# Fewer, larger transfers for the attention stacks, and a new order of the late ones in the SP queue

## The chip, the cores and the metric

One core of a Trainium2 chip runs the whole program. The metric is the device time of one execution in microseconds (us); lower is better.

## The reference

The input x is 2 x 1024 x 256 in f32. xn is its layer norm. The result is x + s * g, where s is attention and g a gated mixture of experts, both fed with xn:

```python
proj = xn @ in_proj.T + in_proj_bias            # q, k, v: 16 heads of 16
scores = einsum('bhqd,bhkd->bhqk', q, k) * SCALE + rel * alibi_slopes   # causal
attn = maximum(softmax(scores), 1e-10)
s = einsum('bhqk,bhkd->bhqd', attn, v) ... @ out_w.T + out_b
# _ffn: rms norm, router over 32 experts, top 4, capacity 128,
#       silu(gate) * up, down, plus a shared expert of 704 columns
g = silu(xn + experts + shared)
x = x + s * g
```

## The kernel before

The work after a prologue is a pipeline over 32 units. Unit k is one attention head (16 heads of batch 0, then 16 of batch 1) and also one expert. Four slots (`SLOTS`) hold the operands of four units. `phases` runs a `phase` function on each engine for k from -2 to 32; on SP the first and the last ones are written out and 24 of them are six turns of a loop over four.

In phase k, in eight steps s, TensorE (PE) does pass 1 of head k + 2 (scores in rows of queries, L765; VectorE takes the row maximum L1342, ScalarE the exponential and its sum L1062), pass 2 of head k (scores again, transposed, with the row's shift as three extra rows of the operand; mask L787, product L791, exponential L1071, clamp L1348) and the values of head k - 1 (L810, L813). Between them lie the expert's steps: transpose of the gathered rows `XE` (L838), gate and up (L850), down (L868), the shared expert (L889, L897).

The precision of f32 is kept with bf16 parts. The operand of a head (`QS`, `KS`, 111 rows of 1024 bf16 in the tile STACKS) is six blocks of 16 rows, taken from the three parts of q or k in DRAM in a fixed order (q: 0, 1, 2, 0, 1, 0; k: 0, 0, 0, 1, 1, 2), and 15 rows for position. The first three of these 15 on the q side are overwritten with the head's shift rows: GpSimd (POOL) works them out, PE flips them (L832), VectorE copies them to CT as 24 rows of 128 (L1361), and SP sends CT to rows 96 to 98 of the stack (`store_shift`, L569). Pass 2 of head k waits for that at its first step (`c_rows_ready`, L775).

All plain loads and stores are issued by SP, one after the other, in the order that is written. In phase k SP issues, each with its wait ahead of it:

1. the stack of head k + 3 (`load_stack`, L497 and L498), after pass 2 of head k - 1;
2. the weights of expert k + 5 (`load_expert`, L514 to L518), after the down product of expert k + 1;
3. in phase 31, the eight loads of the experts' sum (`load_experts_sum`, L610);
4. the attended rows of head k - 1 (`store_heads`, L586), after their copy to OEV (L1407); for the last eight heads they go straight into the tile ATTS (named XN in the profile), for the others to `att_rows` in DRAM;
5. the shift rows of head k + 1 (`store_shift`), after the copy to CT;
6. in phase 25 `load_again(0)`: 1 MB of attended rows of batch 0 into ATTS (L596) and the copy of x of batch 0 to the output, 1 MB from DRAM to DRAM (L597); in phase 26 `load_again(1)`: the attended rows of batch 1 so far (L599) and x of batch 1 (L601).

POOL gathers the rows of expert k + 3 in phase k with an indirect DMA (L1624). In the last phases PE projects the attended rows (L907), the experts' sum is gated on ScalarE and VectorE (`tanh_sum`, `gate`, `last_sum`, L1423), POOL adds the first half to the output and SP stores the second.

In the prologue the bf16 parts of q and k are made in 16 tasks on a ring of four buffers (`RING`) and stored by SP (`store_parts`, L481). A task waits until its buffer's store has landed (L1027). The stores 8 to 11 stand in SP's queue with the stack loads of heads 0 and 1 between them; then come stores 12 to 15, the stacks of heads 2 and 3, and the first four experts.

Of the kernel before, what the change touches and what calls it, by code (L numbers as in the profile page):

```python
# [25 lines left out]
P = 128  # L26
# [5 lines left out]
H = 16  # L32
# [59 lines left out]
DIRECT = UNITS - NQ  # L92

# [14 lines left out]
def build(nc, x, in_proj, in_b, out_w, out_b, slopes, w_norm, w_router, w_gate, w_up, w_down,  # L108
          sw_gate, sw_up, sw_down, w_sg, out):
    ctx = ExitStack()  # L110
    with ctx:
# [316 lines left out]
        def _(sp):  # L428
# [65 lines left out]
            def load_operand(t, rows, plan, alibi, u_head, u, semaphore):  # L494
                one = rows[:, bass.ds(u_head, DH), :]
                for r, part in enumerate(plan):
                    sp.dma_start(t[r * DH:(r + 1) * DH, :], one[part]).then_inc(semaphore, 16)  # L497
                sp.dma_start(t[SHIFT:ROWS, :], alibi[bass.ds(u, 1)].rearrange("a r s -> (a r) s"))\  # L498
                    .then_inc(semaphore, 16)

            def load_queries(u_head, u, slot):
                load_operand(QS[slot], q_parts, (0, 1, 2, 0, 1, 0), q_alibi, u_head, u, stack_loaded[slot])

            def load_keys(u_head, u, slot):
                load_operand(KS[slot], k_parts, (0, 0, 0, 1, 1, 2), k_alibi, u_head, u, stack_loaded[slot])
# [37 lines left out]
            def phase(it, k):  # L543
# [45 lines left out]
            def load_again(b):  # L589

                heads = H if b == 0 else DIRECT
                for r in range(SLOTS):
                    sp.wait_ge(o_stored[r], 64 * (heads // SLOTS + 1))
                if b == 0:
                    sp.wait_ge(moe_started, 32)
                    sp.dma_start(ATTS[:, :, 0, :], att_rows[0:D].rearrange("(a p) t -> p a t", p=P)).then_inc(att_loaded[0], 16)  # L596
                    sp.dma_start(out[0], x[0]).then_inc(x_again[0], 16)  # L597
                else:
                    sp.dma_start(ATTS[:, 0, 1, :], att_rows[D:D + P]).then_inc(att_loaded[1], 16)  # L599
# [1125 lines left out]
```

## Time and profile before

| | us |
|---|---|
| median of 3 runs (lowest, highest) | 638.89 (635.98, 642.01) |
| the profiled execution, own time | 641.21 |
| its span from first to last instruction | 639.6 |
| PE busy | 564.7 (88%) |
| VectorE busy | 489.6 (77%) |
| ScalarE busy | 445.3 (70%) |
| GpSimd busy | 263.8 (41%) |
| granted TensorE clock, mean | 0.961 |

Engines in the rows: PE matmuls, PEld weight loads (they run beside PE), DVE VectorE, ACT ScalarE, POOL GpSimd, SPq the queue of SP, which only issues transfers. What an engine idled for stands in square brackets behind a row, with what ended it.

### The profile page before, as it was taken

The page shows a single profiled execution, that of the slowest core. Times are in us where ns is not written, and L with a number is a line of the kernel's source. Part 1 is how long each engine was busy: PE and PEld are TensorE (multiplying, and loading weights), DVE is VectorE, ACT ScalarE, POOL GpSimd, SP SyncE. Part 2 cuts the span into 40 slices and gives each one's busy share as a digit, 9 for nine tenths or more (in the row PEclk, how much of TensorE's full clock was granted, in tenths as well). Part 3 has the DMA queues.
Part 4 walks back from the last instruction along what each step waited for, and adds up shares of the span by engine and source line. Part 5 has one row for each costly group of instructions (what it writes and reads, how often), then busy time and mean ns, then how long its engine had stood idle before and what let it go on. Part 6 is the DMA issues. An engine that isn't in the chain of part 4 may idle for free.

```text
span 639.6 us, 17284 instructions
## 1 busy us (share of the span) xinstructions
PE 564.7 (88%) x4583; PEld 386.8 (60%) x4584; DVE 489.6 (77%) x1098; ACT 445.3 (70%) x1021; POOL 263.8 (41%) x632
## 2 busy tenths in 40 slices
PE   1699559778998999999999999999999998999994
PEld 1594227545665666666666666666666665666663
DVE  5988963668778778886887788778878885788556
ACT  1412574268877778887888788888878886788670
POOL 7630000215445355445544564455355445344403
PEclk9959869799999999999999999999999999999998
DMA  8992255553335333533543344335334346731157
GB/s 243 179 241 76 97 156 167 136 161 60 91 84 111 86 92 87 107 89 90 102 104 98 87 102 90 87 84 116 90 89 102 92 103 200 167 80 24 16 146 136
DMA packets 79538, 71.47 MB, mean 112 GB/s; under 512 B 18115, under 2 KB 70021, under 8 KB 79493
## 3 DMA queue, kind: packets, MB, share of 16 engines
q1 hardware_dynamic: 70292, 59.30, 34.1%
q0 software_dynamic: 9136, 11.80, 12.3%
q8 instruction: 12, 0.20, 0.1%
q14 instruction: 18, 0.14, 0.1%
q10 hardware_dynamic: 80, 0.03, 0.0%
HBM read 47.82 MB, written 23.59 MB: 112 GB/s over the span
## 4 chain that ended last, share of the span: by engine, by line
PE 50%; ACT 14%; issue 11%; DVE 10%; DMA 7%; SPq 6%; ACTq 1%; POOL 1%; POOLq 0%; DVEq 0%
ACT PSB L1062 7%; PE PSB L897 6%; PE PSB L765 6%; PE PSB L791 6%; ACT PB L1071 5%; PE PSB L889 5%; PE PSB L813 5%; PE PSB L810 4%; PE PSB L868 4%; PE PSB L787 3%; SPq L497 2%; PE PSB L666 2%; PE PSB L761 2%; PE PSB L850 2%; DVE WDS L1277 2%
## 5 line engine op out<-in xcount | busy, mean ns | idle before, releaser
L1342 DVE TENSOR_REDUCE NEGM<-PSB 128x1 f32<-128x1024 f32 (+7 forms) x256 | 192.3, 752 | 64.4 <-PE PSB L765 62.5
L1062 ACT ACTIVATE PSB<-PSB,NEGM 128x1024 f32<-128x1024 f32 (+7 forms) x256 | 182.5, 713 | 33.3 <-DVE NEGM L1342 33.0
L1071 ACT ACTIVATE PB<-PSB 128x128 f32<-128x128 f32 (+7 forms) x256 | 166.3, 651 | 43.7 <-PE PSB L791 41.6
L1348 DVE TENSOR_SCALAR PB<-PB 128x128 f32<-128x128 f32 (+7 forms) x256 | 116.9, 466 | 26.5 <-ACT PB L1071 24.1
L765 PE MATMUL PSB<-STACKS 111*128 111x512 bf16 (+3 forms) x384 | 106.6, 332 | 0.0
L791 PE MATMUL PSB<-STACKS 111*128 111x512 bf16 (+3 forms) x384 | 104.3, 326 | 0.0
L787 PE MATMUL PSB<-MK,IDB 128*128 128x128 bf16 x256 | 57.5, 225 | 21.2 <-ACT PSB L1062 13.7
L1660 POOL DMA_INDIRECT moe_rows<-YE,IDX x32 | 57.3, 1792 | 29.2 <-issue 29.2
L810 PE MATMUL PSB<-PB,VH 128*32 128x256 f32 x640 | 68.3, 387 | 0.0
L787 PEld LDWEIGHTS PSB<-MK,IDB 128*128 128x128 bf16 x256 | 24.5, 96 | 58.4 <-ACT PB L1071 31.5
L761 PE MATMUL PSB<-MQ,IDB 128*128 128x128 bf16 x256 | 58.3, 228 | 1.1 <-ACT UL L1049 0.5
L813 PE MATMUL PSB<-PB,VH 128*32 128x128 f32 x1024 | 55.6, 275 | 0.8 <-DVE PB L1348 0.7
L1620 POOL COPY IDX<-TABS 128x2 int32 (+1 forms) x32 | 20.3, 634 | 79.9 <-DVE VS L1333 79.9
L1624 POOL DMA_INDIRECT XES<-xf_rows,IDX x32 | 38.2, 1193 | 32.5 <-POOL IDX L1620 29.7
L1062 ACT ACTIVATION_READ_ACCUMULATOR PSB<-PSB,NEGM 128x1 f32 x256 | 51.5, 201 | 0.0
L897 PE MATMUL PSB<-SWD,HS 128*128 128x256 f32 x192 | 50.6, 391 | 0.0
L850 PE MATMUL PSB<-WGU,XES 128*128 128x352 f32 x128 | 48.9, 462 | 1.8 <-issue 1.8
L813 PEld LDWEIGHTS PSB<-PB,VH 128*32 128x32 f32 x1024 | 47.1, 109 | 4.6 <-issue 1.4
L1566 POOL TENSOR_TENSOR CR<-LSUM,LEX 128x8 f32<-128x8 f32 x32 | 6.5, 202 | 98.9 <-ACT LEX L1077 98.9
L897 PEld LDWEIGHTS PSB<-SWD,HS 128*128 128x128 f32 x192 | 33.7, 188 | 12.1 <-issue 8.6
L791 PEld LDWEIGHTS PSB<-STACKS 111*128 111x128 bf16 x384 | 32.6, 99 | 12.9 <-issue 0.3
L761 PEld LDWEIGHTS PSB<-MQ,IDB 128*128 128x128 bf16 x256 | 24.7, 97 | 24.5 <-issue 8.9
(199 smaller groups left out, 1169.4 us busy)
## 6 DMA issues: line engine op xcount, KB each, us to landing
STACKS<-q_parts SPq DMA_DIRECT2D x192, 32.0 KB, 1.8
STACKS<-k_parts SPq DMA_DIRECT2D x192, 32.0 KB, 1.8
WGU<-in_L_ffn_w_gate_dram SPq DMA_DIRECT2D x32, 176.0 KB
WGU<-in_L_ffn_w_up_dram SPq DMA_DIRECT2D x32, 176.0 KB
WDS<-in_L_ffn_w_down_dram SPq DMA_DIRECT2D x32, 176.0 KB
q_parts<-PB SPq DMA_DIRECT2D x8, 384.0 KB, 2.6
XN<-in_L_attn_qkv_dram SPq DMA_DIRECT2D x4, 512.0 KB, 6.0
moe_rows<-XN SPq DMA_DIRECT2D x1, 2048.0 KB, 8.7
```

Of the source, the lines that this page charges most:

```text
L761: pe.matmul(psf[:, base + i * P:base + w], IDB[:, :], MQ[:, :], start=True, stop=False, skip_group_check=True)
L765: ins = pe.matmul(psf[:, base + c0:base + c1], q, KS[slot][0:ROWS, c0:c1], start=(c1 < w), stop=True, skip_group_check=True)
L787: pe.matmul(psf[:, base:base + P], IDB[:, :], MK[:, :], start=True, stop=False, skip_group_check=True)
L791: ins = pe.matmul(psf[:, base + c0:base + c1], key, QS[slot][0:ROWS, j * P + c0:j * P + c1], start=(c0 > 0), stop=True, skip_group_check=True)
L810: ins = pe.matmul(o, v, probs[:, c - j:far - j + 1:far - c, :], start=False, stop=(j == 0), skip_group_check=True)
L813: ins = pe.matmul(o[:, 1, :], v, probs[:, far - j, :], start=(far == j), stop=False, skip_group_check=True)
L850: ins = pe.matmul(o[:, 0:2 * F], XET[:, part, :], WGU[slot][:, part, :], start=(part == 0), stop=(part == KC - 1))
L897: ins = pe.matmul(o[:, 0:D], HS[0:m, ch, which * P:(which + 1) * P], SWD[0:m, ch, :], start=(ch == 0), stop=(ch == NF - 1))
L1062: act.activation(sc, sc, ACT.Exp, bias=NEGM[:, par, i:i + 1], accum_out=LSUM[:, par, i:i + 1]).then_inc(exp1_done, 1)
L1071: act.activation(PB[:, k % 2, prob_offset(s):prob_offset(s) + (s + 1) * P], psf[:, base:base + (s + 1) * P], ACT.Exp).then_inc(exp2_done, 1)
L1342: dve.tensor_reduce(NEGM[:, par, i:i + 1], psf[:, base:base + (i + 1) * P], AX_X, ALU.max, negate=True).then_inc(max_ready, 1)
L1348: dve.tensor_scalar(p, p, FLOOR, 0.0, ALU.subtract, ALU.max).then_inc(clamp_done, 1)
```

## The change

Three edits, all in what SP issues:

- A stack operand is loaded in four transfers in place of seven: runs of parts that stand side by side (q: 0-1-2, 0-1, 0) or are repeated (k: 0 three times, 1 twice, 2) become one transfer each, the repeated ones with a source that is broadcast. A whole stack takes 8 in place of 14. The bytes are the same.
- In a phase, `store_shift` stands ahead of `store_heads`, and is one transfer of CT to the three rows in place of three.
- `load_again` becomes five pieces in phases 25 to 29: ATTS of batch 0 in two halves (25, 26), ATTS of batch 1 (27), x of batch 1 in two halves (28, 29). The copy of x of batch 0 becomes eight transfers of 128 rows, one in each phase 2, 6, ..., 30 (`copy_x`), behind the attended rows.

```diff
+AGAIN = range(DIRECT + 1, DIRECT + 6)
-            def load_operand(t, rows, plan, alibi, u_head, u, semaphore):
+            def load_operand(t, rows, runs, alibi, u_head, u, semaphore):
                 one = rows[:, bass.ds(u_head, DH), :]
-                for r, part in enumerate(plan):
-                    sp.dma_start(t[r * DH:(r + 1) * DH, :], one[part]).then_inc(semaphore, 16)
+                r = 0
+                for first, parts, times in runs:
+                    n = parts * times
+                    src = one[first:first + parts]
+                    if times > 1:
+                        src = src.broadcast_to([n, DH, S])
+                    sp.dma_start(t[r * DH:(r + n) * DH, :], src).then_inc(semaphore, 16)
+                    r += n
-                load_operand(QS[slot], q_parts, (0, 1, 2, 0, 1, 0), ...)
+                load_operand(QS[slot], q_parts, ((0, 3, 1), (0, 2, 1), (0, 1, 1)), ...)
-                load_operand(KS[slot], k_parts, (0, 0, 0, 1, 1, 2), ...)
+                load_operand(KS[slot], k_parts, ((0, 1, 3), (1, 1, 2), (2, 1, 1)), ...)
...
+                if exists(it, k + 1):
+                    store_shift(it, k + 1)
                 if exists(it, k - 1):
                     store_heads(it, k - 1)
-                if exists(it, k + 1):
-                    store_shift(it, k + 1)
-                if isinstance(it, int) and k == DIRECT + 1:
-                    load_again(0)
-                if isinstance(it, int) and k == DIRECT + 2:
-                    load_again(1)
+                if k >= 2 and k % SLOTS == 2:
+                    copy_x(it, k)
+                if isinstance(it, int) and k in AGAIN:
+                    load_again(k)
...
-                for a in range(3):
-                    sp.dma_start(rows[SHIFT + a:SHIFT + a + 1, :].rearrange("o (t q) -> o t q", q=P),
-                                 CT[NQ * a:NQ * a + NQ, :]).then_inc(c_rows_ready, 16)
+                sp.dma_start(rows[SHIFT:SHIFT + 3, :], CT[:, :]).then_inc(c_rows_ready, 16)
...
+            def copy_x(it, k):
+                rows = bass.ds(turn(it, k, SLOTS, P), P)
+                sp.dma_start(out[0][rows, :], x[0][rows, :]).then_inc(x_again[0], 16)
+
+            def load_again(k):
+                n = k - AGAIN[0]
+                if n < 3:
+                    heads = D // DH if n < 2 else DIRECT
+                    for r in range(SLOTS):
+                        sp.wait_ge(o_stored[r], 64 * (heads // SLOTS + 1))
+                    sp.wait_ge(moe_started, 32)
+                    sp.dma_start(ATTS[:, n % 2, n // 2, :], att_rows[n * P:(n + 1) * P]).then_inc(att_loaded[n // 2], 16)
+                else:
+                    t = NQ // 2 * (n - 3)
+                    sp.wait_ge(shared_added, 16 * (UNITS // SLOTS // 2))
+                    sp.dma_start(XAGAIN...[:, t:t + NQ // 2, :], x_t[:, NQ + t:NQ + t + NQ // 2, :]).then_inc(x_again[1], 16)
```

The counts that others wait for follow: a stack 8 transfers, shift rows 1, `att_loaded[0]` 2, `x_again[0]` 8, `x_again[1]` 2.

## Rows read from the trace of the kernel before

**Rows 1.** The page's chain that ended last, shares of the span by engine.
```profile
PE 50%; ACT 14%; issue 11%; DVE 10%; DMA 7%; SPq 6%; ACTq 1%; POOL 1%; POOLq 0%; DVEq 0%
```

**Rows 2.** Timeline of DVE, the copy to CT: start us, duration, once a unit.
```profile
202.49 0.21 DVE L1361 COPY CT<-PSB 24x128 bf16<-24x128 bf16 x1 [0.49 <-PE PSB L832]
218.93 0.21 DVE L1361 COPY CT<-PSB 24x128 bf16<-24x128 bf16 x1 [0.49 <-PE PSB L832]
...
309.36 0.21 DVE L1361 COPY CT<-PSB 24x128 bf16<-24x128 bf16 x1 [0.50 <-PE PSB L832]
323.89 0.21 DVE L1361 COPY CT<-PSB 24x128 bf16<-24x128 bf16 x1 [0.49 <-PE PSB L832]
338.25 0.21 DVE L1361 COPY CT<-PSB 24x128 bf16<-24x128 bf16 x1 [0.49 <-PE PSB L832]
353.27 0.21 DVE L1361 COPY CT<-PSB 24x128 bf16<-24x128 bf16 x1 [0.33 <-PE PSB L832]
368.77 0.21 DVE L1361 COPY CT<-PSB 24x128 bf16<-24x128 bf16 x1 [0.50 <-PE PSB L832]
...
531.50 0.21 DVE L1361 COPY CT<-PSB 24x128 bf16<-24x128 bf16 x1 [0.33 <-PE PSB L832]
550.85 0.21 DVE L1361 COPY CT<-PSB 24x128 bf16<-24x128 bf16 x1 [0.49 <-PE PSB L832]
566.17 0.21 DVE L1361 COPY CT<-PSB 24x128 bf16<-24x128 bf16 x1 [0.49 <-issue]
```

**Rows 3.** The chain in order of time at 533 us: start, duration.
```profile
533.20 8.62 DMA XES<-xf_rows,IDX
```

**Rows 4.** Timeline of SP's queue at 534 us.
```profile
534.50 0.62 SPq L597 DMA_DIRECT2D out_dram<-in_L_attn_qkv_dram  x1
```

**Rows 5.** Timeline of SP's queue at 201 us.
```profile
200.96 3.42 SPq L586 DMA_DIRECT2D att_rows<-OEV  x4
```

**Rows 6.** Who waited for the shift rows (L569) in all.
```profile
  PEld PSB L787: 8.8, 16
  PE PSB L787: 3.6, 4
```

**Rows 7.** Timeline of SP's queue in the prologue.
```profile
91.83 2.93 SPq L497 DMA_DIRECT2D STACKS<-q_parts  x6
```

**Rows 8.** The chain in order of time, store 11 of the parts.
```profile
103.55 4.27 DMA k_parts<-XES
```

**Rows 9.** Waits of PE over the whole span: total, times, longest.
```profile
PE PSB L733 <- DVE TS L1326: 2.0, 1, 2.0
```

**Rows 10.** Timeline of PEld, the first expert's gate and up.
```profile
130.66 0.30 PEld L850 LDWEIGHTS PSB<-WGU,XES 128*128 128x128 f32 x2 [2.31 <-issue]
```

**Rows 11.** Windows: PE, PEld, DVE, ACT, POOL busy, clock, DMA share of 16 engines, GB/s.
```profile
111.00:113.00 2.00, 2.00 (x11) 1.67 (x10) 2.00 (x2) 1.59 (x4) 0.00 (x0) 1.00 1.01 342
344.00:348.00 4.00, 4.00 (x29) 2.78 (x28) 3.64 (x8) 3.26 (x9) 0.88 (x5) 1.00 0.28 67
```

**Rows 12.** The tile XES, 320 to 335 us: one gather, its use, its landing.
```profile
L838 PEld LDWEIGHTS PSB<-IDF,XES x2: 141/142/143, 330.7 to 330.9; 128*128 128x128 f32 x2
L1624 POOL DMA_INDIRECT XES<-xf_rows,IDX x1: 1090/1090/1090, 326.2 to 326.2; - x1
DMA to landing us min/median/max: 3.1/3.1/3.1
```

**Rows 13.** Timeline of SP's queue at the end.
```profile
604.64 3.11 SPq L586 DMA_DIRECT2D XN<-OEV  x4
607.86 2.08 SPq L569 DMA_DIRECT2D STACKS<-CT  x3
610.07 3.98 SPq L610 DMA_DIRECT2D XFT<-moe_rows  x8
```

**Rows 14.** Timeline of DVE at the end.
```profile
606.93 0.21 DVE L1361 COPY CT<-PSB 24x128 bf16<-24x128 bf16 x1 [1.12 <-PE PSB L832]
619.23 0.69 DVE L1423 TENSOR_TENSOR XFT<-XFT,XNT 128x512 f32<-128x512 f32 x1 [0.79 <-DMA XFT<-moe_rows]
```

More of the change, by code:

```diff
@@ L501, in load_queries @@
             def load_queries(u_head, u, slot):
-                load_operand(QS[slot], q_parts, (0, 1, 2, 0, 1, 0), q_alibi, u_head, u, stack_loaded[slot])
+                load_operand(QS[slot], q_parts, ((0, 3, 1), (0, 2, 1), (0, 1, 1)), q_alibi, u_head, u, stack_loaded[slot])
             def load_keys(u_head, u, slot):
-                load_operand(KS[slot], k_parts, (0, 0, 0, 1, 1, 2), k_alibi, u_head, u, stack_loaded[slot])
+                load_operand(KS[slot], k_parts, ((0, 1, 3), (1, 1, 2), (2, 1, 1)), k_alibi, u_head, u, stack_loaded[slot])
             def load_stack(u_head, u, slot):
@@ L587, in store_heads @@
                         .then_inc(o_stored[k % SLOTS], 16)
[L589 to L594, printed above, removed]
+            def copy_x(it, k):
[7 more added lines that the diff above has]
+                        sp.wait_ge(o_stored[r], 64 * (heads // SLOTS + 1))
                     sp.wait_ge(moe_started, 32)
-                    sp.dma_start(ATTS[:, :, 0, :], att_rows[0:D].rearrange("(a p) t -> p a t", p=P)).then_inc(att_loaded[0], 16)
-                    sp.dma_start(out[0], x[0]).then_inc(x_again[0], 16)
+                    sp.dma_start(ATTS[:, n % 2, n // 2, :], att_rows[n * P:(n + 1) * P]).then_inc(att_loaded[n // 2], 16)
                 else:
-                    sp.dma_start(ATTS[:, 0, 1, :], att_rows[D:D + P]).then_inc(att_loaded[1], 16)
+                    t = NQ // 2 * (n - 3)
                     sp.wait_ge(shared_added, 16 * (UNITS // SLOTS // 2))
-                    sp.dma_start(XAGAIN.rearrange("p (t d) -> p t d", d=D), x_t[:, NQ:2 * NQ, :]).then_inc(x_again[1], 16)
+                    sp.dma_start(XAGAIN.rearrange("p (t d) -> p t d", d=D)[:, t:t + NQ // 2, :],
+                                 x_t[:, NQ + t:NQ + t + NQ // 2, :]).then_inc(x_again[1], 16)
             def load_experts_sum():
@@ L623, in _ @@
             sp.wait_ge(added_out, 16 * (NT // 4))
-            sp.wait_ge(x_again[0], 16)
+            sp.wait_ge(x_again[0], 16 * (UNITS // SLOTS))
         @block.tensor
@@ L750, in pass1 @@
                 if s == 0:
-                    pe.wait_ge(stack_loaded[slot], turn(it, k, SLOTS, 14 * 16, 14 * 16))
+                    pe.wait_ge(stack_loaded[slot], turn(it, k, SLOTS, 8 * 16, 8 * 16))
                 used = {0: -1, 1: 0, 2: 1, 3: 2, 4: 3, 5: 3, 6: 5, 7: 4}[s]
@@ L774, in pass2 @@
                 if s == 0:
-                    pe.wait_ge(c_rows_ready, unit(it, k, 48, 48))
+                    pe.wait_ge(c_rows_ready, unit(it, k, 16, 16))
                 if s == 4 and ahead:
@@ L914, in project @@
                     pe.wait_ge(exp1_done, UNITS * NQ)
-                    pe.wait_ge(att_loaded[0], 16)
+                    pe.wait_ge(att_loaded[0], 32)
                 if g == 1:
@@ L1359, in turn_shift @@
                 if k >= 1:
-                    dve.wait_ge(c_rows_ready, unit(it, k, 48))
+                    dve.wait_ge(c_rows_ready, unit(it, k, 16))
                 dve.tensor_copy(CT[:, :], PSB[0:3 * NQ, O_BANK, C_COL:C_COL + P // 2].bitcast(BF16))\
@@ L1442, in add_input @@
                 x_late = XAGAIN[:, 512 * n:512 * (n + 1)]
-                dve.wait_ge(x_again[1], 16)
+                dve.wait_ge(x_again[1], 32)
                 dve.wait_ge(fin_product, n + 1)
@@ L1693, in _ @@
             phases(pool, phase, 1)
-            pool.wait_ge(x_again[0], 16)
+            pool.wait_ge(x_again[0], 16 * (UNITS // SLOTS))
             out_t = out.rearrange("b (t p) d -> p (b t) d", p=P)
```

## The prediction

> **What bounds the kernel now.** I read the chain of waits first: half of it is PE's own work, ScalarE and VectorE carry 24%, and DMA with SP's queue 13% [rows 1]. So transfers are no bound of the whole, but there are places where they are. To find them I took one instruction that runs once a unit, the copy to CT, and read the distances [rows 2]. In the steady part four distances repeat: 14.53 (309.36 to 323.89), 14.36, 15.02 and 15.50 us. There the chain holds PE, ScalarE and VectorE, and a faster SP gives nothing. Three places do not fit:
> - 531.50 to 550.85 is 19.35 us where 15.50 is the rule (353.27 to 368.77), and 550.85 to 566.17 is 15.32 where 14.53 is: 3.85 + 0.79 = 4.6 us.
> - 202.49 to 218.93 is 16.44 where 14.36 is the rule (323.89 to 338.25): 2.1 us.
> - the prologue and the end, which have no rhythm and are read by their waits.
>
> **Part 1, the late loads and the copy of x in pieces.** At 533.20 a gather of expert rows takes 8.62 us [rows 3], where one takes 3.1 [rows 12]; 1 us behind it SP issues the two 1 MB transfers [rows 4], and PE then waits for the gather. The second lot (1.5 MB) follows a unit later. After the change phase 25 has 0.5 MB, phase 26 0.6 MB, and each comes after four issues of attended rows, so at about CT + 4 us, when the gather, issued at CT + 1.7 [rows 2, 3] and landed 3.1 us later, is nearly through. At 342 GB/s [rows 11] half a megabyte is 1.5 us of all engines; the gather has 1.4 us to spare even in a steady unit (issue 326.2, landed 3.1 later, used at 330.7 [rows 12]). So nothing is late next, and I count the whole 4.6 us; if half of the collision stays, 2.3. The pieces cost SP issues of up to 0.6 us each [rows 4] in a queue that waits for CT every unit; their cover is that wait, and it only fails at the end (part 4).
>
> **Part 2, the shift first and as one transfer.** In the steady part the attended rows are ready before CT and are issued in SP's idle time, so the order is free there. At 202.49 CT is made, but SP is busy with attended rows from 200.96 for 3.42 us [rows 5], 0.86 for an issue where a stack issue takes 0.49 [rows 7]: the queue itself paused, for 1.5 us. The shift left 1.7 us late and PE stood for it. In all PE idled 3.6 us in 4 places for them and its weight loads 8.8 us in 16 [rows 6]. With the shift first, its issue is the first thing after CT; two issues fewer, of 2.08 / 3 = 0.7 us each [rows 13], make it land 1.4 us earlier. That removes the 2.1 us of that unit; the small waits of the weight loads (some 0.4 us each) lie beside a product of pass 1 that is still running, and I count them at nothing (bound: 1 us in all). A pause of 1.5 us may now fall on the shift itself; it has 1.4 - 0.4 = 1.0 us of slack then, so I take 2.0 us, and 0 if pauses fall badly. What is queued behind the shift's wait on SP are the attended rows, wanted only four units later by VectorE, and the next stack, which waits for pass 2 and is not ready earlier.
>
> **Part 3, the stack in 8.** A stack issue in the prologue is 2.93 / 6 = 0.49 us [rows 7], so an operand of 7 is 3.4 us and one of 4 is 1.9. In the steady part that only lengthens SP's waits. In the prologue it is on the chain: stores 9, 10, 11 stand behind one operand each, store 11 leaves at 103.55 and lands at 107.82 [rows 8], ScalarE's last part waits for it, then VectorE's sum over xn, and PE waits 2.0 us for that sum [rows 9]. Three operands save 4.5 us ahead of store 11, more than the 2.0 that PE can use, since its products for v run until then. The first expert is behind all four stacks: 24 issues less are some 11 us, and the wait of PE for its weights before 130.66 [rows 10] (2.3 us on the weight side; I count 1.5, for matmuls run into it and ScalarE and VectorE come up behind) goes. That is 3.5 us, if the larger transfers move as fast as the small ones.
> This is the unknown: no transfer of the trace has three or two leading copies of 16 rows. If one of three copies is moved by only three of the 16 engines (and one of two by two), the busiest takes 32 + 32 + 2 + 2 = 68 KB of an operand, 69.6 kB. An engine at work moves 342 / (1.01 x 16) = 21 GB/s in the busiest stretch of the prologue, and 67 / (0.28 x 16) = 15 GB/s where only single small stack transfers run [rows 11]. At 21 an operand is 3.3 us there, about what the issues took before. Then store 11 (three operands, three stores of 24.6 kB at 1.2 us, from 93.3, where I put the end of store 8's data, some 2 us after its issue, which is the one ahead of 91.83) lands at 107.5, 0.3 us earlier than now. The first expert (eight operands, seven stores, its own 34 kB) lands at 130.5, where it was 130.66. The prologue then gives 0.3 us. At 15 it lands at 145 and costs 14. I take 1.9 us for the prologue, between 3.5 and 0.3: the transfers of a crowded engine are long runs of rows, nearer to the busy row than to the quiet one.
> The Trainium skill, DMA: Bandwidth & Descriptors, section Rules for kernel authors, speaks against the form: an outermost dimension of size c below 16, such as a leading broadcast of c copies, confines the whole DMA to at most c engines. The profile's rows do not tell engines apart, so nothing here shows it yet; by it the prologue would give 0.3 us and not 3.5. The same section's advice to coalesce small transfers speaks for the change.
>
> **Part 4, the end.** SP issued attended rows from 604.64 (3.11 us), shift rows (2.08) and at 610.07 the eight loads of the experts' sum [rows 13]. After: the shift waits for CT (606.93 + 0.21 [rows 14]), leaves at 607.2 and takes 0.7; then the four attended transfers, 2.6 without a pause; then `copy_x` of phase 30, 0.5. The sum's loads start at 611.0 and not 610.07, 1.0 us later, behind 128 KB of copying (0.3 us). VectorE already stood 0.79 us for the last of these loads [rows 14], and works without a pause from there to the last head's values. So 1.3 us are lost; 0.5 if SP's pause of 0.5 in the attended rows does not recur, 2 if the loads crowd.
>
> **Sum.** -4.6 - 2.0 - 1.9 + 1.3 = -7.2 us. The profiled execution took 641.21 itself (span 639.6), so it would be 634.0. The median is 2.3 lower, 638.89; so 631.7.
>
> **Rivals.**
> - A, SP's pauses fall on the shift or in front of it wherever it stands, and part 2 gives nothing: -5.2, 633.7. For it: nothing in [rows 5] ties the pause to the attended rows. Against: SP is idle ahead of CT, so a pause has where to fall.
> - B, the stack's long runs on few engines hold up the gather, which is issued shortly ahead of the first stack transfer. One run of 16 rows, 33 kB, at 21 GB/s is 1.6 us against 1.4 to spare: 0.2 x 28 = 5.6 us, sum -1.6, 637.3. For it: at 533 the gather did wait behind loads issued after it [rows 3, 4]. Against: where the gather's own data come first, nothing happens.
> - C, slower: few engines, at the quiet row's rate. The prologue's transfers queue on the first engines. The expert's data need 8 x 69.6 + 7 x 24.6 + 34 = 763 kB of the busiest one; at 15 GB/s that is 51 us from 93.3, so 145.0 with the landing, and PE stands 14.3 us longer. -4.6 - 2.0 + 14.3 + 1.3 = +9.0, 647.9. It decides from 18.2 GB/s downward (there the prologue's loss eats the rest). Against it: the 21 of the busy row, and that the quiet row counts an engine's start for each single row, which a run would share.
> - D, few engines, but at the busy row's rate: the prologue gives 0.3 us. -4.6 - 2.0 - 0.3 + 1.3 = -5.6, 633.3. For it: one operand's issues and one operand's data on the busiest engine are then equally long, so the queue only changes its place. Against: the rows show no transfer that would be split so. The Trainium skill (DMA: Bandwidth & Descriptors, Rules for kernel authors), as told in part 3, gives this case.
> - E, the late pieces still collide with the gathers of phases 25 and 26: half of part 1 stays, -4.9, 634.0.
>
> **How the numbers follow.** The forecast 0.36, with part 3 anywhere from 3.5 to 1 (-8.8 to -6.3, 630.1 to 632.6); A 0.13, B 0.11, C 0.09, D 0.24, E 0.07. Runs of one kernel here spread over 3 us to either side. 1% of the median, 6.4 us, is about what a measurement of this kernel can tell from no change: faster is below 632.5. The forecast lies 0.8 us inside it, D 0.8 outside. Three quarters of the forecast (0.27), two fifths of D (0.10) and a fifth of A, B and E (0.06) count as faster, C as slower, the rest as the same: 0.43, 0.48, 0.09. The range leaves C out: from 630.1 less 3.6 for the runs' spread and small waits to B and its spread, 626.5 to 640.
>
> **What would show it.** The distance at the copy of CT in phases 25 and 26 should be 15.5 and 14.5; gathers should land in 3.1 to 3.5; no wait on the shift rows above 0.5 us; an operand's issue in the prologue 1.9 us; PE's wait for the sum over xn gone, and most of that for the first expert; the loads of the experts' sum some 3.9 us behind CT. If stack transfers of 96 KB take 3 us or more to land, few engines carry them. I am wrong if the steady distances of 14.36 to 15.50 change by even 0.3 us, for there are 28 of them, or if the first expert comes later than PE asks.

## The result, and the profile after

| | us |
|---|---|
| before, median of 4 runs (lowest, highest) | 638.9 (635.98, 642.01) |
| after, median of 4 runs (lowest, highest) | 632.6 (632.48, 632.87) |
| ratio, 95% interval | 0.9898 (0.9866 to 0.9929) |
| the profiled execution of after, its span, mean granted clock | 632.87, 630.9, 0.963 |

6.3 us less. In this table and below, a ratio to before compares fast executions only; three unchanged ones (643.21 in e5, 640.48 and 644.38 in the last group), over 1.5% above the fastest of their kernel, stand in the medians and ranges but not in the ratios. The two profiled spans are 8.7 us apart, 639.6 and 630.9. The page's chain that ended last, by engine, answers to [rows 1]:

```profile
PE 53%; ACT 16%; issue 11%; DVE 10%; DMA 6%; SPq 3%; ACTq 1%; DVEq 0%; POOLq 0%; POOL 0%
```

SP's queue halved its share, 6 to 3%; but a second profile of before (e5) has 3% too, so the halving can't be put down to the change. The copies to CT in the timeline of VectorE answer to [rows 2]:

```profile
199.00 0.21 DVE L1372 COPY CT<-PSB 24x128 bf16<-24x128 bf16 x1 [0.41 <-PE PSB L843]
213.52 0.21 DVE L1372 COPY CT<-PSB 24x128 bf16<-24x128 bf16 x1 [0.50 <-PE PSB L843]
...
480.98 0.21 DVE L1372 COPY CT<-PSB 24x128 bf16<-24x128 bf16 x1 [0.49 <-PE PSB L843]
495.29 0.21 DVE L1372 COPY CT<-PSB 24x128 bf16<-24x128 bf16 x1 [0.41 <-PE PSB L843]
...
524.73 0.21 DVE L1372 COPY CT<-PSB 24x128 bf16<-24x128 bf16 x1 [0.33 <-PE PSB L843]
540.22 0.21 DVE L1372 COPY CT<-PSB 24x128 bf16<-24x128 bf16 x1 [0.49 <-PE PSB L843]
554.51 0.21 DVE L1372 COPY CT<-PSB 24x128 bf16<-24x128 bf16 x1 [0.41 <-PE PSB L843]
```

The distance from one copy to the next is called a turn below. The pauses are gone: 15.49 and 14.29 us in phases 25 and 26 where [rows 2] has 19.35 and 15.32, and 14.52 where it has 16.44. The unit that took 14.53 takes 14.31 now (480.98 to 495.29).

The prologue did not get shorter, although the queue did. Its lines are of the chain that ended last:

```profile
98.47 5.81 DMA k_parts<-XES
...
116.25 6.10 DMA XES<-xf_rows,IDX
```

and this one is of PE's timeline, at the end of the wait for that gather:

```profile
122.40 0.69 PE L849 MATMUL PSB<-IDF,XES 128*128 128x128 f32 x2 [4.71 <-DMA XES<-xf_rows,IDX]
```

Store 11 leaves 5.1 us sooner (98.47, was 103.55 [rows 8]; 3.0 of it measured from store 8) but needs 5.81 us to land in place of 4.27. The first gather of expert rows takes 6.10 us, where one takes 3.1 [rows 12], and PE stands 4.71 us for it (1.0 in before). The second gather takes 7.06 us, but its rows are used only 14.4 us behind its issue.

The end got longer. SP's timeline answers to [rows 13], VectorE's to [rows 14]:

```profile
595.88 0.78 SPq L575 DMA_DIRECT2D STACKS<-CT  x1
596.78 2.57 SPq L591 DMA_DIRECT2D XN<-OEV  x4
599.39 0.59 SPq L597 DMA_DIRECT2D out_dram<-in_L_attn_qkv_dram  x1
600.10 4.10 SPq L621 DMA_DIRECT2D XFT<-moe_rows  x8
```

```profile
609.60 0.69 DVE L1434 TENSOR_TENSOR XFT<-XFT,XNT 128x512 f32<-128x512 f32 x1 [2.52 <-DMA XFT<-moe_rows]
```

The loads of the experts' sum start 4.5 us behind the copy to CT (595.58), where they started 3.1 behind it, and VectorE's wait for them is 2.52 us, where it was 0.79.

Before and after can be cut at four marks: the issue of store 8 in the prologue (91.40 before, 89.28 after), the first copy to CT, the copy of phase 23 (number 24 from 0) and the last copy. Every kernel of this study is cut that way, which the text below refers to as the table of stretches. Each value is a difference of two such start times, the last one the span less the last copy.

| kernel | store 8 to first copy | copies 0 to 24 | copies 24 to 31 | last copy to end | span |
|---|---|---|---|---|---|
| before, first profile | 52.5 | 358.1 | 104.9 | 32.7 | 639.6 |
| before, second profile (e5) | 53.2 | 355.7 | 100.2 | 33.4 | 630.8 |
| e1, late loads in pieces alone | 51.9 | 357.2 | 100.8 | 33.7 | 634.4 |
| e2, shift alone | 52.1 | 354.2 | 100.0 | 33.9 | 629.8 |
| e3, stacks in 8 alone | 51.5 | 355.2 | 101.1 | 32.7 | 630.4 |
| after, first profile | 51.8 | 354.3 | 100.3 | 35.3 | 630.9 |
| after, second profile (e6) | 53.1 | 354.1 | 100.4 | 35.6 | 632.0 |
| e7, after with an earlier sum | 51.7 | 354.2 | 100.4 | 32.2 | 628.4 |
| e4, after with interleaved rows | 47.9 | 354.2 | 100.0 | 36.0 | 628.6 |
| e8, both | 47.6 | 354.2 | 100.0 | 32.7 | 624.9 |
| e9, e8 without the pieces | 47.5 | 354.2 | 100.0 | 33.5 | 626.1 |
| e10, e8 with the shift behind | 47.4 | 354.1 | 100.3 | 32.1 | 625.2 |
| e11, e8 with stacks in 14 | 51.8 | 354.4 | 100.1 | 32.1 | 627.6 |
| e12, e9 with the loads at the gather | 47.8 | 354.1 | 102.2 | 33.8 | 627.4 |

Between the first profiles of before and after, 2.1 us of the 8.7 lie ahead of store 8, where nothing was changed. The rest is -0.8 - 3.8 - 4.6 + 2.7 = -6.5 us.

### The profile page after: what moved, and what is told of

Read it like the earlier page. It is cut to its first block, busy times and chain, and to the rows that moved or that the text cites. A ratio compares the mean times of both kernels' runs of the same rounds, so it can differ in the third digit from the quotient of the medians.

```text
span 630.9 us, 16914 instructions
## 1 busy us (share of the span) xinstructions
PE 559.0 (89%) x4584; PEld 385.3 (61%) x4584; DVE 489.6 (78%) x1098; ACT 444.4 (70%) x1021; POOL 263.1 (42%) x632
## 4 chain that ended last, share of the span: by engine, by line
PE 53%; ACT 16%; issue 11%; DVE 10%; DMA 6%; SPq 3%; ACTq 1%; DVEq 0%; POOLq 0%; POOL 0%
ACT PSB L1073 9%; PE PSB L908 7%; PE PSB L776 6%; PE PSB L802 6%; ACT PB L1082 6%; PE PSB L900 5%; PE PSB L824 5%; PE PSB L821 4%; PE PSB L879 4%; PE PSB L798 3%; PE PSB L772 2%; PE PSB L677 2%; DVE WDS L1288 2%; PE PSB L861 2%; DMA XN<-in_L_attn_qkv_dram 1%
## 5 line engine op out<-in xcount | busy, mean ns | idle before, releaser
L1073 ACT ACTIVATION_READ_ACCUMULATOR PSB<-PSB,NEGM 128x1 f32 x256 | 51.5, 201 | 0.0
L908 PEld LDWEIGHTS PSB<-SWD,HS 128*128 128x128 f32 x192 | 33.7, 188 | 12.1 <-issue 8.6
```

Of the source, the lines that this page charges most:

```text
L908: ins = pe.matmul(o[:, 0:D], HS[0:m, ch, which * P:(which + 1) * P], SWD[0:m, ch, :], start=(ch == 0), stop=(ch == NF - 1))
L1073: act.activation(sc, sc, ACT.Exp, bias=NEGM[:, par, i:i + 1], accum_out=LSUM[:, par, i:i + 1]).then_inc(exp1_done, 1)
```

## The experiments

Times of one group stand beside runs of before on the same chip: 634.8 us (629.6 to 638.6, 31 runs) for e1 to e4, 638.0 (633.6 to 640.8, 23 runs) for e5 to e8, 636.9 (630.5 to 644.4, 17 runs) for e9 to e12. Of two kernels of different groups only ratios to before, or stretches, are compared.

**e1, the late loads and the copy of x in pieces, nothing else.** Before, with this:

```diff
-                if isinstance(it, int) and k == DIRECT + 1:
-                    load_again(0)
-                if isinstance(it, int) and k == DIRECT + 2:
-                    load_again(1)
+                if k >= 2 and k % SLOTS == 2:
+                    copy_x(it, k)
+                if isinstance(it, int) and k in AGAIN:
+                    load_again(k)
```

> Only the late loads and the copy of x in pieces, on the kernel before. The theory that the parts add up: 4.9 us come back in phases 25 and 26 (distances of the copies to CT 15.5 and 14.5 or a little less), nothing changes ahead of them, and the end loses about 1 us, since the copy of phase 30 stands ahead of the loads of the experts' sum (0.6 us of issue and 0.3 us of data): ratio to before about 0.994. The rival, that a good part of the gain of the whole change is the state of the run and not these pieces: under 2 us, ratio above 0.997.

Measured 636.6 us (634.4 to 640.0, 12 runs), ratio 1.0026 (0.9999 to 1.0053). No gain, against the expectation. The turn of phase 25 was 15.50 us, as expected. Its gather still took 5.42 us to land behind half a megabyte issued 0.9 us after it, but PE used the rows only 6.3 us behind its issue. The gather of phase 27 took 5.26 us, was used 5.3 us behind its issue, and that turn was 15.02 us where other kernels have 14.4.

**e2, the shift rows first and as one transfer, nothing else.** Before, with this:

```diff
+                if exists(it, k + 1):
+                    store_shift(it, k + 1)
                 if exists(it, k - 1):
                     store_heads(it, k - 1)
-                if exists(it, k + 1):
-                    store_shift(it, k + 1)
...
+                sp.dma_start(rows[SHIFT:SHIFT + 3, :], CT[:, :]).then_inc(c_rows_ready, 16)
```

> Only the shift rows as one transfer and ahead of the attended rows, on the kernel before. If the gain of some 3 us in the first two turns of the loop and the steady 0.16 us per turn belong to the shift, both are seen here: the copies to CT at 14.3, 14.4, 15.0, 15.5 us distance, no unit of 16.4 us; the end is later by 0.7 us, as the loads of the sum now wait for CT and four issues: about -3 us, ratio 0.995. The rival: the 16.4 us unit is made by the long queue of 14 stack issues, and remains here; then about -0.5 us, ratio 0.999.

Measured 633.6 us (631.5 to 638.0, 12 runs), ratio 0.999 (0.996 to 1.0021): a miss too. But the turn of phase 25 was 15.50 us here as well, with all 2 MB still loaded in it. With the shift first, the two loads come 2.3 and 2.8 us behind the gather, and it lands in 3.50 us.

**e3, the stacks in 8 transfers, nothing else.** Before, with the new `load_operand` and the count of 8.

> Only the stacks in 8 transfers, on the kernel before. If 48 rows in one transfer are moved by three engines: the first gather lands in 6 us or more and PE waits 4 us or more for it, the wait for the first expert shrinks to about 0.3 us, the sum over xn comes in time, and the whole is worth -1 to 0 us, ratio 0.998 to 1. The rival, that all engines share such a transfer and the slow first gather has another cause: the stack rows leave in 0.5 us bursts of 200 GB/s or more, and the whole is worth -3.5 us, ratio 0.994.

Measured 634.8 us (632.0 to 637.5, 12 runs), ratio 1.0002 (0.9976 to 1.0027). That is what the theory of few engines expected, and the first gather took 6.27 us here too. The turn of phase 25 was 15.83 us, again without an edit that touches it; the gather of that phase landed 6.58 us behind its issue, with the loads 0.9 and 1.3 us behind it as in before.

So each part alone ran without the pause of [rows 3], and none was faster than before. e2 has a reason to cure it, the greater distance between gather and loads, and e1 has one in part; e3 has none. Either the parts cure one pause three times, or before does not always have it. e5 asks that.

**e4, after with the rows interleaved.** The same bytes in the same 8 transfers, but the part index is the second dimension of the source and no longer the outermost one: 16 rows outside, 1 to 3 parts inside. The rows of a stack block stand in another order; both operands hold the parts in the matching order, so the sum over rows is the same.

```diff
-                    src = one[first:first + parts]
+                    src = one[first:first + parts].rearrange("a d s -> d a s")
                     if times > 1:
-                        src = src.broadcast_to([n, DH, S])
+                        src = src.broadcast_to([DH, times, S])
```

> The kernel after, with the rows of a stack interleaved: row 3 d + c of the first 48 holds copy c of row d, so that the source's outermost dimension is the 16 rows and not the copies; bytes, transfers and waits are the same. The theory of few engines: the stack transfers now spread over 16 engines, the first gather lands in 3.1 to 3.6 us, its wait of 4.7 us falls to 1, the first expert's wait goes: 3 to 4 us under the kernel after, ratio to before 0.984 to 0.986. The rival, that the gather is slowed by the denser stream of stack bytes however it is spread: no change against the kernel after, ratio 0.990.

Measured 630.2 us (627.5 to 631.3, 8 runs), ratio 0.992 (0.9884 to 0.9957): the fastest of its group, but the expected ratio of 0.984 to 0.986 was missed. After itself did not run on this chip, so its runs can't be set beside these. In the profile the first gather landed in 3.61 us, as expected. In the table of stretches the prologue is 47.9, where the kernels without this edit have 51.5 to 53.2; copies 0 to 24 are as in after.

How many engines carry such a transfer is not named in any row, but the trace tells it in two ways. It has one record for each step by which a landing transfer raises its semaphore, and the DMA view gives a time to landing only where there are 16 of them per transfer. For the transfers of 48 rows it gives none in after (first line) and 2.5 us with the rows outside (second line, e8):

```profile
STACKS<-q_parts SPq DMA_DIRECT2D x32, 96.0 KB
```

```profile
STACKS<-q_parts SPq DMA_DIRECT2D x32, 96.0 KB, 2.5
```

Counted in the trace, the 64 transfers of one slot have 1024 such records in e8, 16 each, and 624 in after: 78 per stack in place of 128, so that the four merged transfers of a stack have 14 together, not 64. And of the 2 KB packets of one stack (issued from 336.1 us in after, 333.0 us in e8), two or three are in flight for 4.4 of the 6.5 us that they take together in after, and the last ends 3.2 us behind the last issue; in e8 they take 4.7 us together, with two or three in flight for only 0.5 of them and mostly more, and the last ends 1.6 us behind the last issue.

**e5, before itself, with a profile.**

> The kernel before, unchanged, with a profile on the chip of the other runs. Theory (the pause of phase 25 is a race: the gather of that phase is issued only 1.3 us ahead of the 2 MB of loads, needs 6.5 us to be in time, and in the profiled execution took 8.6): this profile may show the turn of phase 25 anywhere between 15.5 and 19.3 us, and its time follows it; at the 634.8 us that before has on this chip, some 2 us or less of the pause of 3.8 is left, and the four first turns after head 3 (15.94, 16.44 and 15.48 us in the first profile) are shorter too. Rival (the pauses belong to the kernel, and the first profile differs by the prologue alone): turns of 19.3 and 16.4 us again, and the 4 to 6 us less stand ahead of the first copy to CT at 143.9 us.

Measured 638.0 us (632.5 to 643.2, 12 runs). The profiled execution took 632.48 us, 8.7 less than the first profiled one of the same kernel. The timeline of VectorE, copies to CT:

```profile
199.71 0.21 DVE L1361 COPY CT<-PSB 24x128 bf16<-24x128 bf16 x1 [0.49 <-PE PSB L832]
214.15 0.21 DVE L1361 COPY CT<-PSB 24x128 bf16<-24x128 bf16 x1 [0.49 <-PE PSB L832]
...
526.54 0.21 DVE L1361 COPY CT<-PSB 24x128 bf16<-24x128 bf16 x1 [0.33 <-PE PSB L832]
542.07 0.21 DVE L1361 COPY CT<-PSB 24x128 bf16<-24x128 bf16 x1 [0.50 <-PE PSB L832]
556.59 0.21 DVE L1361 COPY CT<-PSB 24x128 bf16<-24x128 bf16 x1 [0.49 <-PE PSB L832]
```

14.44 us where [rows 2] has 16.44, 15.53 where it has 19.35, 14.52 where it has 15.32. The gather of phase 25 and what SP issued behind it, from the timelines of GpSimd and SP, and PE's use of the rows:

```profile
528.25 1.53 POOL L1624 DMA_INDIRECT XES<-xf_rows,IDX  x1 [0.99 <-POOL IDX L1620]
```

```profile
529.13 0.38 SPq L596 DMA_DIRECT2D XN<-att_rows  x1
529.54 0.62 SPq L597 DMA_DIRECT2D out_dram<-in_L_attn_qkv_dram  x1
```

```profile
534.59 0.40 PE L838 MATMUL PSB<-IDF,XES 128*128 128x128 f32 x2
```

The two big loads follow the gather by 0.9 and 1.3 us, exactly as in [rows 3, 4] (534.08 and 534.50 behind 533.20). PE uses the rows 6.34 us behind the gather's issue. Here the gather landed 6.26 us behind it, just in time: PE's weight load waited 0.20 us, its product not at all. In [rows 3] it took 8.62 us and PE stood 2.2; in e3, at the same distance, 6.58 us, and PE stood 0.1. With the same distance the gather sometimes wins and sometimes loses. The theory stands and the rival falls: only 2.4 of the 8.8 us between the two profiles lie ahead of the first copy to CT.

**e6, after itself on the same chip.**

> The changed kernel, unchanged, on the chip of the other runs, against before there. Theory (the three parts remove the same pauses, so their gains do not add up; each alone gave a ratio of 0.999 to 1.003 here): ratio 0.990 to 0.998, about 631 to 633 us. Rival (the parts help one another, and the ratio is that of the first chip): 0.987 to 0.990, 627 to 629 us.

Measured 634.1 us (632.2 to 638.3, 12 runs), ratio 0.9956 (0.9927 to 0.9985). The gain is there but half of the first one. Laid beside e5's profile its span is 1.2 us longer, 632.0 against 630.8: 1.5 us gained in copies 0 to 24, 2.1 lost at the end, nothing in the prologue. Against this one execution of before without pauses, the change gives nothing in the profile.

**e7, after with the experts' sum loaded sooner.** The eight loads stand behind the shift rows of head 31, ahead of the attended rows, and `copy_x` moves one phase up. These are two edits at once, and no run takes them apart.

```diff
-                if isinstance(it, int) and k == UNITS - 1:
-                    load_experts_sum()
                 if exists(it, k + 1):
                     store_shift(it, k + 1)
+                if isinstance(it, int) and k == UNITS - 2:
+                    load_experts_sum()
...
-                if k >= 2 and k % SLOTS == 2:
+                if k >= 1 and k % SLOTS == 1:
                     copy_x(it, k)
```

> The changed kernel with the eight loads of the experts' sum right behind the shift rows of head 31, and with every part of the copy of x one phase earlier, so that none stands in the last phases. Theory (the end of after is 2.7 us longer than that of before because those loads start 4.5 us behind the copy to CT in place of 3.1, VectorE waits 2.5 us for them, and TensorE, idle meanwhile, is granted 1.2 GHz sooner): loads at 1.0 us behind the copy, VectorE's wait 0, end from the last copy to CT 35.3 down to 31.5 to 32.7, ratio to the changed kernel 0.995 (3 us less). Rival (the end is set by the projection's chain and the clock alone, which falls in any case): loads earlier, end still above 34.5, ratio 0.998 to 1.

Measured 631.8 us (630.4 to 634.2, 6 runs), ratio 0.9906 (0.9876 to 0.9936); against e6, 631.8 / 634.1 = 0.996. The end was 32.2 us, as expected. Two rows, of SP's and of VectorE's timeline:

```profile
598.99 3.98 SPq L621 DMA_DIRECT2D XFT<-moe_rows  x8
```

```profile
608.23 0.69 DVE L1434 TENSOR_TENSOR XFT<-XFT,XNT 128x512 f32<-128x512 f32 x1 [0.52 <-DMA XFT<-moe_rows]
```

The loads start 2.8 us behind the copy to CT (596.20), not 1.0: they now wait for the last experts' rows to reach DRAM. That still cuts VectorE's wait from 2.52 to 0.52 us. Busy time by stretch, for after (the first two lines) and for this kernel (the last two), each pair from 21.9 and 21.4 us ahead of the end. The columns are length, busy time of PE, its weight loads, VectorE, ScalarE and GpSimd, granted clock, DMA share, GB/s:

```profile
609.00:615.00 6.00, 3.58 (x61) 2.62 (x58) 5.40 (x10) 4.00 (x7) 0.00 (x0) 1.00 0.02 6
...
621.00:627.00 6.00, 5.40 (x15) 4.03 (x13) 4.21 (x7) 0.00 (x0) 0.00 (x0) 0.62 0.84 175
```

```profile
607.00:613.00 6.00, 5.58 (x65) 4.03 (x66) 5.48 (x11) 5.70 (x10) 0.00 (x0) 1.00 0.09 22
...
619.00:625.00 6.00, 4.73 (x15) 3.48 (x13) 4.63 (x7) 0.00 (x0) 0.00 (x0) 0.72 1.00 195
```

In after PE is idle for 2.4 of 6 us: it waits for VectorE's clamp of the last head, which comes late behind VectorE's own wait. The stretch with the projection that follows has 0.62 of full speed; in e7 PE is idle for 0.4, and it has 0.72. The last 16 matmuls of the projection show the price, in after and in e7:

```profile
619.96 6.44 PE L918 MATMUL PSB<-OWT,XN 128*128 128x256 f32 x16 [3.46 <-DMA XN<-OEV]
```

```profile
618.35 5.38 PE L918 MATMUL PSB<-OWT,XN 128*128 128x256 f32 x16 [3.23 <-DMA XN<-OEV]
```

That is 1.1 us on top of the 2.0 of the wait, and together the 3.1 us by which the end is shorter. That PE's idle time lowers the clock is not shown by this. In after, e1, e4 and e12 the clock stood at the lower of its two levels for 6.8 us ahead of or in the projection, with PE idle for 2.42, 0.81, 3.06 and 0.93 us some 18 us ahead of the end; in before, e2, e8 and e9 it did so for 3.4 us, with PE idle for 0.70, 1.52, 0.82 and 1.23.

**e8, both.** The edits of e4 and e7.

> The same end, with the rows of the stack loads interleaved as well (outermost dimension 16 in place of 1, 2 or 3). Both effects stand in different stretches (prologue, end), so they should add up: the interleaved kernel ran at 630.2 us, 0.992 of before; with 3 us less at the end 627 us, ratio 0.987. Rival of the clock (an earlier end only moves the fall of the granted clock): 629.5 us.

Measured 625.2 us (624.6 to 626.8, 6 runs), ratio 0.9794 (0.9766 to 0.9823), the fastest kernel of the study and faster than the expected 627 us; against e6, 625.2 / 634.1 = 0.986. Against e7 on the same chip the interleaving alone gives 6.6 us in the medians, 4.1 in the first stretch of the profiles; where the rest comes from is open. The chain of this kernel between 96 and 126 us holds no transfer. Two lines of it, where after had the lines of store 11 and of the gather:

```profile
112.73 0.80 PE PSB L744 x8
...
114.02 1.96 PE PSB L750 x16
```

Most of that stretch is PE's own products. The table of stretches shows the parts add up: 47.6 and 32.7 us, the middle unchanged.

**e9, e8 without the pieces.** The late loads and the copy of x whole, in phases 25 and 26, behind the attended rows as in before.

> The best kernel so far (interleaved rows, experts' sum loaded right behind the last shift rows) with the late loads and the copy of x put back whole, as before: 2 MB in phase 25 and 1.5 MB in phase 26, behind the attended rows. Theory (the gather of that phase only loses when the loads are issued within some 1.3 us of it; behind shift and attended rows they come 2.8 us later, when it is through, so the pieces are worth nothing once the shift goes first): turn of phase 25 within 0.3 us of 15.5, and the time within 1.5 us of the best kernel, 625.2. Rival (2 MB in one phase cost what part 1 said, wherever they start): turns of phases 25 and 26 together 2 to 4.6 us longer, 627.5 to 630 us.

Measured 626.9 us (626.3 to 627.8, 6 runs), ratio 0.9851 (0.9806 to 0.9896). The turns of phases 25 and 26 are 15.49 and 14.30 us: with the shift first, 2 MB in one phase disturb nothing. SP's and GpSimd's timelines show why:

```profile
523.27 2.61 SPq L590 DMA_DIRECT2D XN<-OEV  x4
526.07 0.44 SPq L600 DMA_DIRECT2D XN<-att_rows  x1
526.55 0.60 SPq L601 DMA_DIRECT2D out_dram<-in_L_attn_qkv_dram  x1
```

```profile
523.71 1.53 POOL L1628 DMA_INDIRECT XES<-xf_rows,IDX  x1 [0.99 <-POOL IDX L1624]
```

The loads come 2.4 and 2.8 us behind the gather, when it is nearly through. Only the end is 0.8 us longer than in e8; there the loads of the sum start 3.6 us behind the copy to CT (2.7 in e8), after SP waited 2.4 us for the last experts' rows to land.

**e10, e8 with the shift behind the attended rows.** Still one transfer.

```diff
-                if exists(it, k + 1):
-                    store_shift(it, k + 1)
-                if isinstance(it, int) and k == UNITS - 2:
-                    load_experts_sum()
                 if exists(it, k - 1):
                     store_heads(it, k - 1)
+                if exists(it, k + 1):
+                    store_shift(it, k + 1)
+                if isinstance(it, int) and k == UNITS - 2:
+                    load_experts_sum()
```

> The best kernel so far with the shift rows behind the attended rows again (still one transfer). Theory (the order matters where the attended rows are late or SP's queue pauses; the repeated 0.12 to 0.15 us per turn of four that the changed kernel gained in the steady part come from fewer shift transfers, not from the order): steady turns unchanged at 14.31 and 14.41, 0 to 1.5 us slower than the best kernel's 625.2 and more spread. Rival (the order gives the steady gain): turns of 14.5 once in four, and 1 to 3 us slower.

Measured 626.8 us (626.0 to 627.3, 6 runs), ratio 0.9847 (0.9802 to 0.9892). It ran on another chip than e8, whose ratio of 0.9794 is lower, but the two intervals overlap; e9, on the same chip, took 626.9. The turns of the steady part stay at 14.31 and 14.41 us; one, of phase 26, is 14.57 in place of 14.31. Its gather landed in 4.78 us, with a load issued close to it again, and PE's weight load waited for it. The spread is no wider than e8's. So the steady gain comes from the one transfer, and the order is worth 0.3 us in this profile, through the gather.

**e11, e8 with the stacks in 14.**

> The best kernel so far with the stacks in 14 transfers of 16 rows as before. Theory (fewer transfers help only if each still reaches all 16 engines: the prologue gains 3 to 3.5 us that way, and nothing when they are confined): first copy to CT 3.5 us later than the 137.9 of the best kernel, 628 to 629.5 us, ratio to the best 1.005. Rival (the interleaving helps the gathers of the steady part too): more than 4 us slower, with part of it behind the first copy to CT.

Measured 632.3 us (629.2 to 634.5, 12 runs), ratio 0.9937 (0.9909 to 0.9966). The profiled execution, 629.34, has the first copy 3.2 us later than e8 and everything behind it alike, which is the theory. But the median lies 3.0 us above that execution. The kernels with 8 interleaved transfers and the earlier sum (e8, e9, e10) never spread by more than 2.2 us over 6 runs, this one spread by 5.3 over 12. It is 5.5 us above e10 on the same chip, more than the 3.2 us of the profile. Where the slower executions lose it, the one profile does not show.

**e12, e9 with the late loads at the gather.** The loads of phase 25 stand ahead of the attended rows and so come close to the gather. Those of phase 26 stay behind, although the expectation speaks of both.

```diff
+                if isinstance(it, int) and k == DIRECT + 1:
+                    load_again(0)
                 if exists(it, k - 1):
                     store_heads(it, k - 1)
-                if isinstance(it, int) and k == DIRECT + 1:
-                    load_again(0)
```

> The kernel without the pieces, with the loads of phases 25 and 26 moved ahead of the attended rows, so that they are issued within 1 us of the gather in every execution. Theory (this is what happens in some executions of the kernel before and not in others): the gather of phase 25 lands 6.5 to 9 us after its issue, TensorE waits for it, turn of phase 25 17 to 19.5 us, time 2 to 4.5 us above the kernel without the pieces and more spread than it. Rival (the pause of the first profile came from something else): turns as in the kernel without the pieces, time within 1 us of it.

Measured 629.0 us (626.0 to 630.4, 6 runs), ratio 0.9879 (0.9829 to 0.9928), 2.1 us above e9, its runs 4.4 us apart where e9's are 1.5. The timelines of SP, GpSimd, PE and VectorE:

```profile
522.24 0.38 SPq L600 DMA_DIRECT2D XN<-att_rows  x1
522.68 0.64 SPq L601 DMA_DIRECT2D out_dram<-in_L_attn_qkv_dram  x1
```

```profile
522.59 1.53 POOL L1628 DMA_INDIRECT XES<-xf_rows,IDX  x1 [0.99 <-POOL IDX L1624]
```

```profile
531.10 0.44 PE L842 MATMUL PSB<-IDF,XES 128*128 128x128 f32 x2 [2.00 <-DMA XES<-xf_rows,IDX]
```

```profile
520.89 0.21 DVE L1365 COPY CT<-PSB 24x128 bf16<-24x128 bf16 x1 [0.34 <-PE PSB L836]
538.59 0.21 DVE L1365 COPY CT<-PSB 24x128 bf16<-24x128 bf16 x1 [0.39 <-PE PSB L836]
```

One load is 0.35 us ahead of the gather, one 0.1 behind; the gather lands 8.46 us behind its issue, PE waits 2.0 us for the rows and the turn is 17.70 us, 2.2 longer than in e9. So loads close to the gather make the pause; at the distance of before, 0.9 us, they make it in some executions only. The spread was wider too, in 6 runs each.

## Why the prediction was right, and where its steps were not

The forecast of 631.7 us for a measured 632.6 came out of four terms. Parts 3 and 4 together took back 2.5 us more than forecast, and the first turns and the steady part gave 1.8 us more. That these nearly cancel is luck. So is part of the agreement of the medians: the pauses of parts 1 and 2 were read in one execution and taken off the median, although no run shows that the median execution has them.

**Part 1, -4.6 us: right in the profiled execution, not a property of the kernel.** The turns of phases 25 and 26 lost 3.86 and 1.03 us. But the step "I count the whole 4.6 us" took one execution's pause for every one's. e5 shows an execution of before without it; e12 shows that loads close to the gather make it; e2 and e9 show that, once the shift goes first, whole loads cost no turn, since the attended rows now stand between gather and loads (2.3 us or more). The pieces by themselves gained nothing in e1, whose end is also 0.3 to 1.0 us longer than the two of before. That different shares of paused executions make the two ratios, 0.9898 on the first chip and 0.9956 on the chip of e6, is likely but not shown.

**Part 2, -2.0 us: mechanism half right, size right.** The unit of 16.44 us became 14.52, a gain of 1.9. Yet e5's before has 14.44 there, so this too was a pause of one execution. What is lasting is the term that was counted at nothing with a bound of 1 us, the small waits of the steady part. The prediction said that a change of the steady distances by 0.3 us would prove it wrong; one in four changed by 0.2. Copies 0 to 24 take 354.1 to 354.4 us in every kernel with one shift transfer and 355.2 or more with three, so it is 0.8 us at least and 1.5 against e5. e10 puts it on the one transfer; the order has no part in it.

**Part 3, -1.9 us: the step that failed.** From store 8 to the first copy to CT the four profiles with 8 transfers as changed (e3, e6, e7 and the first of after) took 51.5 to 53.1 us, the five with 14 (e11 among them) 51.8 to 53.2: no gain that these can show. This is rival D, with its 0.3 us, and the choice of 1.9 "nearer to the busy row" was wrong. e4, e8, e9, e10 and e12, with the rows outermost in the source, take 47.4 to 47.9. e4 differs from after, and e8 from e7, in nothing else: 3.9 and 4.1 us less, the "3.5 us, if the larger transfers move as fast as the small ones", and more. By the Trainium skill, DMA: Bandwidth & Descriptors, section Rules for kernel authors, an outermost dimension below 16 confines a transfer to at most that many engines; these runs agree with it, with 4.1 us for that edit alone and 14 landing records in place of 64 for the merged transfers of a stack, though no row names the engines. The wait in which it shows is the one rival B named, a gather held up by the stack's long runs: it happened to the first two gathers (6.10 and 7.06 us), of which PE waited for the first, not to the 28 steady ones, whose turns did not get longer. With the rows outermost the first gather takes 3.6 to 4.4 us, but the second still 6.5 to 7.5. Rival C fell: a packet of 2 KB took 103 ns on average in that part of after, 20 GB/s and not 15, and no first expert came 14 us late. Two sizes were off as well. An operand's issues take 2.5 us (2.03 + 0.44), not 1.9, and the first expert's issue came 5.7 us sooner counted from store 8 (28.8 for 34.5), not some 11.

**Part 4, +1.3 us: mechanism right, size too small.** The loads of the sum were to come 1.0 us later against the copy to CT; they came 1.4 later, and VectorE's wait grew by 1.7 us. What the step left out is the clock: the last 16 matmuls of the projection took 6.44 us, with 6.8 us at the lower level, and 5.38 in before, with 3.4. Why the lower level lasted longer is open (e7). The end grew by 2.7 us against the first profile and 1.9 against the second. The parts alone have 33.7 (pieces, e1), 33.9 (order, e2) and 32.7 (stacks, e3); the two of before are 0.7 apart themselves, so no single part is shown to lengthen it.

**The sum.** Predicted for the profiled execution -4.6 - 2.0 - 1.9 + 1.3 = -7.2. The profiled executions differ by 8.3 us (641.21 and 632.87), of which about 2.1 lie ahead of store 8, where nothing was changed. Measured in the stretches behind it, -6.5: -4.9 for part 1; -3.8 in copies 0 to 24, of which 1.9 are part 2's unit, the rest the steady gain and other turns that were long in one execution; -0.8 in the prologue, inside the spread of unchanged kernels there (51.8 to 53.2); +2.7 at the end, and 0.3 in a turn ahead of it. The range held. Rivals A and E fell with the turns of 14.52, 15.49 and 14.29 us: no pause came back on the shift, none of the collision stayed. The chance of "faster" by over 1% was 0.43 and of "within 1%" 0.48; the ratio of 0.9898 lies on the bound between them, and the second chip's 0.9956 on the side of "same".

**What stays open.** Unchanged kernels vary from execution to execution by more than any profile here shows: e6 over 6.1 us, e11 over 5.3, before over 9.5 in the last group, even without its two longest. The collision of gather and loads is worth at most some 5 us of it; a turn was lost to it by 3.9 us in the first profile of before, 2.2 in e12 and 0.3 in e3, and by 0.6 in phase 27 of e1. How often before pauses was not counted: only two of its executions have a profile. Why kernels with many small stack transfers spread more than those with 8 interleaved ones was not tried.

## What to carry to other kernels

A pause in one profile is one execution. Before it enters a sum at full size, ask by how much the late transfer missed its use; here the use came 6.3 us behind the issue and the gather took 6.3 to 8.6, so the same code showed 0 and 3.9 us, and an edit that left the gather alone (e3) seemed to cure it. When small transfers are merged, look at the outermost dimension of the merged form: parts outside and rows inside gave nothing, rows outside and parts inside gave 4.1 us with the same bytes and count. Moving an urgent issue to the front moves the others back, so read the last turn by itself: what the queue does in its idle time everywhere else stood on the path there, and VectorE's wait grew by 1.7 us.

## What was not expected of the hardware

- A gather on GpSimd's queue is slowed by loads that SP issues after it: 6.26, 6.58 and 8.62 us with 2 MB issued 0.9 to 1.3 us behind it (e5, e3, before), 3.1 alone, and 3.4 to 3.5 with the loads 2.3 us or more behind (e2, e9).
- The cost of an SP issue of a stack transfer depends on its form. In the prologue the medians are 0.74 us for 48 rows, 0.64 for 32 and 0.43 for 16 in after; 0.58 for each of the three in e8, with the parts inside; and 0.42 to 0.56 for a block of 16 rows in before. So four issues in place of seven save 0.9 us of queue (2.03 + 0.44 against 2.93 + 0.43), not 1.5.
- A packet of 2 KB of the stack loads took 84 ns (median) in after and 98 ns in before, read from the packets of the trace; that is 24 GB/s for a packet. The mean of 103 ns in the prologue of after gives 20, close to the 21 of the prediction.
- An idle time of PE of 2.4 us in 6, some 6 us ahead of the projection, went with a granted clock of 0.62 in it; 0.4 us of idle time went with 0.72. But e1 had the longer stretch at the lower level with 0.8 us of idle time there, and e2 the shorter one with 1.5.
